# Flamingo block on one core: turned maxima ahead of the slot's extra products, values behind the first transposed scores, PSUM copies one slot later

## The chip, the cores and the metric

The kernel runs on one core of a Trainium2 chip. The metric is the device time of one execution in microseconds (us). The kernel before takes 424.69 us (median of 3 runs, 424.21 to 425.44).

## The reference

The input is `x` of 32 samples with 128 rows of 128 features, and for each sample a context of 77 rows. First a gated cross attention with 16 heads of 8 features, then a gated mixture of experts (one shared expert, and 3 of 15 routed ones for each row):

```python
query, key_, value = proj(layernorm(x), w_q), proj(ctx, w_k), proj(ctx, w_v)     # 16 heads of 8
attn = softmax(query @ key_.T / sqrt(8))
x = x + tanh(g_xattn) * ((attn @ value) merged @ w_o.T)
h = layernorm(x)
shared = gelu(h @ sW1 + sb1) @ sW2 + sb2
topv, topi = top_k(softmax(h @ gW + gb), 3)
routed = sum over the 3 chosen experts of topv * (gelu(h @ rW1[e] + rb1[e]) @ rW2[e] + rb2[e])
x = x + tanh(g_ffn) * (shared + routed + h)
```

## The kernel before

Each engine has an instruction stream written out by hand; semaphores tie them together. There is no scheduler: an engine does its instructions in the order of the code, and an instruction whose semaphore is not there yet holds up all behind it on that engine.

The first part is a loop over the 32 samples, one slot each: `for t in range(B)`, with `g, o = divmod(t, 4)`, so eight groups of four slots, o = 0 to 3. Each engine has its own copy of this loop. In slot t the core part of the attention is pipelined over several samples:

- TensorE (PE): `turn_max(t)` (L1315) transposes the row maxima of the scores of sample t into PSUM; `scores(t+1, 0..3)` (L1305) are the scores of the next sample, one product for each head group, in two PSUM banks used in turn; `turn_on` (L1358), `values(t-1)` (L1342), `scores_t(t, 0..3)` (L1325), the transposed scores of sample t with the maxima as further rows of one operand, also in two banks; `project(t-2)` (L1362), `turn_o(t-1)` (L1353).
- ScalarE (ACT): `max_rows(t)` (L695) copies the turned maxima out of PSUM into `q_stack`, where `scores_t(t, ..)` reads them; `exps(t, 0..3)` (L703); `onT_leaves`, `oT_leaves`.
- VectorE (DVE): `maxima(t+1, 0..3)` (L894) of the scores, on which `turn_max(t+1)` waits; `residual(t-2)` (L911), `invert`, `normalise`, `stats2_of`.

Beside this core each slot has extras, which differ with o. On PE: o = 0 `front_v(g+1)` (L1280) and `token_logits(g-2)` (L1381); o = 1 `front_x(g+2)` (L1263, in the middle of the slot) and `front_q(g+2)` (L1270); o = 2 `front_k(g+2)` (L1254) and `ranks(g-2)` (L1390 to L1394); o = 3 `turn_x2(g-1)` (L1373). Their results are copied out of PSUM by ACT (`lead_q` L668, `lead_k` L655, `x2T_leaves` L686) and DVE (`trail_q` L881, `trail_k` L877, `v_leaves` L887, `add_bias` L931, `place` L963). SyncE (SP) sends q and k to DRAM once they are complete (`send_q`, `send_k`) and loads them back in another layout for the group after next (`load_k`, `load_q` L381).

Two more chains pass through the loop. The second layer norm: `var2_of(g-1)` (L920, DVE), `pow2(g-1)` (L542 and L544, GpSimd (POOL), a power of -1/2) and `shift2_of(g-1)` (L927, DVE), the last two in slot o = 2; `shift2_of` stands ahead of `maxima(t+1, 2)` on DVE. The weights of the first expert layer: nine pieces, in each of them `lead_w1` (L720, ACT), then on POOL `trail_w1`: a subtraction (L557) and the load of the piece after next (L562). A piece comes every third slot, at t = 3, 6, ..., 27.

POOL also scatters normalised rows to the experts' areas in DRAM (L551), three in a slot from the last slot of group 2 on. POOL's loop is, in order:

```python
if o == 3 and g + 3 < NG: pow1(g + 3)
if o == 2 and g >= 1: pow2(g - 1)
if s >= 0:
    pool.wait_ge(exp_done, t * HG + 1);       scatter(s, m, m + 1)
    pool.wait_ge(exp_done, t * HG + 2)
    pool.wait_ge(max_done, (t + 1) * HG + 3); scatter(s, m + 1, m + 2)
    pool.wait_ge(exp_done, t * HG + 4);       scatter(s, m + 2, m + 3)
if t % 3 == 0 and 1 <= t // 3 <= PIECES: trail_w1(t // 3 - 1)
```

The second scatter of a slot thus waits for `maxima(t+1, 2)`, the third for `exps(t, 3)`.

After the loop come 76 blocks of routed expert work (L1434 to L1464), the shared expert, and gathers on POOL (L618) that bring the experts' rows back.

Of the kernel before, what the change touches and what calls it, by code (L numbers as in the profile page):

```python
# [17 lines left out]
def flamingo_kernel(nc, x, ctxT, g_xattn, g_ffn, wqT, wkT, wvT, woT, w1_chunks, b1_cols, sW2, w2_experts, b2, sb2,  # L18
                    gW, gb, ident, picks, consts, out):
    B, S, D = x.shape  # L20
# [10 lines left out]
    NG = B // GB  # L31
# [20 lines left out]
    ROUTE = 11  # L52
    PIECES = -(-NCH // 4)
    TABLE_AT = HALF * GB + 9

# [5 lines left out]
    with ExitStack() as ctx:  # L61
# [149 lines left out]
        zeroed = sem("zeroed")  # L211
# [309 lines left out]
        def _(pool):  # L521
# [59 lines left out]
            for t in range(B):  # L581
                g, o = divmod(t, GB)
# [8 lines left out]
                if s >= 0:  # L591
# [3 lines left out]
                    if t < B - 1:  # L595
# [4 lines left out]
                        scatter(s, m + 2, m + 3)  # L600
                if t % 3 == 0 and 1 <= t // 3 <= PIECES:
                    trail_w1(t // 3 - 1)

# [46 lines left out]
        def _(act):  # L650
# [94 lines left out]
            for t in range(B):  # L745
                g, o = divmod(t, GB)
                ahead = g + 2 < NG
                max_rows(t)
                if t >= 2:
                    onT_leaves(t - 2)  # L750
                if t >= 1:
                    oT_leaves(t - 1)
                exps(t, 0)
                exps(t, 1)
                if o == 1 and ahead:
                    xT_leaves(g + 2)
                if o == 0 and ahead:
                    apply1(g + 2, 0, 2)
                if o == 3 and 1 <= g < NG:
                    apply2(g - 1, 2, GB)  # L760
                if t == 0:
                    lead_q(1)
                exps(t, 2)
                exps(t, 3)
                if t == 0:
                    act.wait_ge(q_lo_ready, 2)
                    act.dma_start(qd[1], q_parts[:].bitcast(F32)).then_inc(q_sent, 16)
                if o == 0 and ahead:
                    apply1(g + 2, 2, GB)
                if o == 1 and ahead:  # L770
                    lead_q(g + 2)
                if o == 1 and g >= 2:
                    exp_logits(g - 2)
                if o == 2 and ahead:
                    lead_k(g + 2)
                if o == 2 and 1 <= g < NG:
                    apply2(g - 1, 0, 2)
                if o == 3 and g >= 1:
                    x2T_leaves(g - 1)
                if t % 3 == 0 and 1 <= t // 3 <= PIECES:  # L780
                    lead_w1(t // 3 - 1)

# [18 lines left out]
            def pad_rows(h, e):  # L801
                row = act.value_load(pad_row[0:1, h * E + e:h * E + e + 1], min_val=0, max_val=2 * HALF_ROWS - BLK)
                act.dma_start(xd[bass.ds(row, BLK), :].rearrange("(p c) d -> p (c d)", c=BC), zeros[:, 0:BC * D]).then_inc(pads_in[h], 16)

            lead_rows(0)
            lead_rows(1)
# [46 lines left out]
        def _(dve):  # L853
# [211 lines left out]
            for t in range(B):  # L1065
                g, o = divmod(t, GB)
                ahead = g + 2 < NG
                if t + 1 < B:
                    maxima(t + 1, 0)
                    maxima(t + 1, 1)  # L1070
                if o == 0 and ahead:
                    shift1_of(g + 2)
                if o == 1 and g >= 2:
                    choose(g - 2)
                if o == 2 and 1 <= g < NG:
                    var2_of(g - 1)
                if o == 2 and g >= 2:
# [5 lines left out]
                if t >= 2:  # L1083
                    residual(t - 2)
                if o == 2 and 1 <= g < NG:
                    shift2_of(g - 1)
# [3 lines left out]
                if t == 0:  # L1090
                    trail_q(1)
                    dve.wait_ge(tanh_done, 1)
                if 1 <= t <= B:
                    invert(t - 1)
                    normalise(t - 1)
                if o == 0 and g < NG - 1:
                    v_leaves(g + 1)
                if o == 1 and ahead:
                    trail_q(g + 2)
                if o == 2 and ahead:  # L1100
                    trail_k(g + 2)
                if t >= 2:
                    stats2_of(t - 2)
                if o == 3 and g >= 2:
                    weigh(g - 2)
                if o == 2 and g >= 2:
                    place(g - 2)
                if o == 2 and g + 3 < NG:
                    stats1_of(g + 3)
                    var1_of(g + 3)  # L1110
                if t >= B - NX + 1:
                    stage(t - (B - NX + 1))
                if o == 0 and g >= 2:
                    add_bias(g - 2)
                if t in (TABLE_AT, TABLE_AT + 1):
# [133 lines left out]
        def _(pe):  # L1249
# [206 lines left out]
            def layer2(u):  # L1456
# [9 lines left out]
                ins.then_inc(l2_done, 1)  # L1466

            for t in range(B):
                g, o = divmod(t, GB)
                ahead = g + 2 < NG  # L1470
                turn_max(t)
                if t + 1 < B:
# [4 lines left out]
                if t >= 2:  # L1477
                    turn_on(t - 2)
                if o == 1 and g >= 2:
                    pe.wait_ge(route_step, (g - 2) * ROUTE + 1)  # L1480
                if o == 3 and g >= 2:
                    pe.wait_ge(route_step, (g - 2) * ROUTE + 7)
                if t >= 1:
                    values(t - 1)
                scores_t(t, 0)
                scores_t(t, 1)
                if o == 1 and ahead:
# [12 lines left out]
                if t >= 1:  # L1500
                    turn_o(t - 1)
                if o == 0 and g < NG - 1:
                    front_v(g + 1)
# [7 lines left out]
                if o == 2 and g >= 2:  # L1511
                    if g == 2:
                        pe.wait_ge(zeroed, 2)
                    ranks(g - 2)
# [137 lines left out]
```

## Time and profile before

| | |
|---|---|
| runs | 424.69 us median (424.21 to 425.44) |
| profiled execution | 424.94 us, span 422.8 us |
| PE busy | 373.8 us, 88% |
| DVE, ACT, POOL busy | 295.8, 275.1, 267.2 us |
| the loop over samples, first `turn_max` to the last | 24.0 to 190.2 us of the span |

Busy times of one engine say how much of the span it worked; the rows of a timeline give the start and length of each instruction (those alike in a row are merged, xN), and in brackets how long the engine had sat idle before it and which instruction ended that. A matmul's row reaches to its modelled end, so that PE's pace is read from start to start.

### The profile page before, as it was taken

The numbers are of one execution on the slowest core, as the hardware profiler recorded it, in microseconds if no ns is written. First come the engines' busy times: TensorE is split into PE (matmuls) and PEld (weight loads), VectorE is DVE, ScalarE is ACT, GpSimd is POOL, SyncE is SP. The second block draws the span as 40 slices with busy tenths as digits, with TensorE's granted clock in tenths as the row PEclk, the third lists the DMA queues.
The fourth block names the chain that finished last, engine by engine and source line by source line (L and its number), as shares of the span: only waits on it lengthen the run. The fifth ranks groups of instructions, "written<-read, shape, count | busy, mean of one in ns | idle before, by whom it ended". The sixth has DMA issues, their size and how long they took to land.

```text
span 422.8 us, 12465 instructions
## 1 busy us (share of the span) xinstructions
PE 373.8 (88%) x3840; PEld 333.6 (79%) x3840; DVE 295.8 (70%) x968; ACT 275.1 (65%) x609; POOL 267.2 (63%) x263
## 2 busy tenths in 40 slices
PE   3379899989999989999899988899999999999940
PEld 1257778778787878877899987799999997999930
DVE  4546767687878768776668977678767762687862
ACT  4248799889889877977666654466666666354400
POOL 8920313357868767774987987406777776777771
PEclk9859999999999999999999999999999999999985
DMA  4457865638373637744345547656666652224232
GB/s 127 128 132 203 275 156 165 193 96 232 112 210 116 190 102 233 272 140 153 118 159 175 150 139 225 220 173 187 198 196 188 194 156 82 76 76 106 76 79 63
DMA packets 57463, 66.30 MB, mean 157 GB/s; under 512 B 9300, under 2 KB 48340, under 8 KB 57400
## 3 DMA queue, kind: packets, MB, share of 16 engines
q1 hardware_dynamic: 49224, 49.17, 39.3%
q0 software_dynamic: 6800, 14.46, 11.8%
q10 hardware_dynamic: 1376, 1.88, 1.4%
q8 instruction: 33, 0.54, 0.6%
q14 instruction: 30, 0.25, 0.2%
HBM read 35.63 MB, written 29.29 MB: 154 GB/s over the span
## 4 chain that ended last, share of the span: by engine, by line
PE 53%; POOL 16%; issue 7%; DMA 6%; DVE 5%; ACT 5%; SPq 3%; ACTq 2%; POOLq 0%; DVEq 0%
PE psum L1464 13%; POOL k_heads L618 8%; PE psum L1325 8%; PE psum L1342 6%; PE psum L1444 4%; PE psum L1445 3%; PE psum L1446 3%; PE psum L1305 3%; PE psum L1434 3%; POOL q_stack L618 2%; ACT probs L703 2%; DMA q_stack<-q_split 2%; DVE max_cols L894 2%; DMA w_raw<-rows_by_expert 2%; POOL rstd L544 2%
## 5 line engine op out<-in xcount | busy, mean ns | idle before, releaser
L551 POOL DMA_INDIRECT rows_by_expert<-xn_all,row_of x96 | 95.3, 993 | 35.7 <-issue 19.0
L798 ACT ACTIVATE probs<-psum,b1c 128x256 f32<-128x256 f32 x152 | 63.7, 470 | 26.3 <-PE psum L1446 25.4
L1464 PE MATMUL psum<-w_all,probs 128*128 x608 | 80.1, 275 | 0.0
L1464 PEld LDWEIGHTS psum<-w_all,probs 128*128 128x128 f32 x608 | 74.2, 191 | 0.2
L703 ACT ACTIVATE probs<-psum 77x512 f32<-77x512 f32 x128 | 68.8, 587 | 5.9 <-PE psum L1325 4.5
L618 POOL DMA_INDIRECT k_heads<-outs_by_block,back_row x60 | 58.3, 972 | 22.0 <-issue 16.2
L894 DVE TENSOR_REDUCE max_cols<-psum 128x4 fp32r<-128x312 f32 x128 | 55.2, 472 | 9.5 <-PE psum L1305 9.4
L1325 PE MATMUL psum<-q_stack,k_heads 128*77 128x128 f32 x512 | 55.1, 244 | 1.5 <-ACT q_stack L695 1.4
L1325 PEld LDWEIGHTS psum<-q_stack,k_heads 128*77 128x77 f32 x512 | 43.7, 150 | 14.5 <-issue 6.1
L1032 DVE CAST w_ring<-w 128x512 fp32r x76 | 34.7, 456 | 22.1 <-issue 20.6
L1444 PE MATMUL psum<-q_parts,w_ring 128*128 128x256 f32 x152 | 49.0, 323 | 1.1 <-DVE q_parts L1020 1.1
L787 ACT ACTIVATE q_parts<-psum 128x256 fp32r<-128x256 f32 x76 | 29.0, 384 | 27.2 <-PE psum L1434 26.7
L1305 PE MATMUL psum<-k_heads,q_stack 128*128 128x312 f32 x128 | 35.3, 357 | 9.8 <-DMA q_stack<-q_parts 6.7
L1445 PE MATMUL psum<-q_parts,w_ring 128*128 128x256 f32 x152 | 42.7, 281 | 0.0
L1446 PE MATMUL psum<-q_parts,w_ring 128*128 128x256 f32 x152 | 42.7, 281 | 0.0
L1020 DVE TENSOR_TENSOR q_parts<-psum,q_parts 128x256 fp32r<-128x256 f32 x76 | 31.8, 420 | 11.6 <-ACT q_parts L787 9.1
L618 POOL DMA_INDIRECT v_pad<-outs_by_block,back_row x24 | 23.5, 980 | 23.8 <-DMA outs_by_block<-probs 15.1
L1040 DVE TENSOR_TENSOR probs<-psum,probs 128x256 f32<-128x256 f32 x76 | 31.9, 420 | 7.3 <-PE psum L1464 3.1
L1342 PE MATMUL psum<-probs,v_pad 128*32 128x128 f32 x1024 | 34.6, 276 | 2.1 <-DVE placed L963 1.9
L1434 PE MATMUL psum<-ident_sb,w_raw 128*128 128x128 f32 x152 | 29.7, 278 | 5.7 <-DMA w_raw<-rows_by_expert 5.6
L1342 PEld LDWEIGHTS psum<-probs,v_pad 128*32 128x32 f32 x1024 | 26.0, 109 | 8.5 <-issue 4.5
L1580 PEld LDWEIGHTS psum<-w_shared,probs 128*128 128x128 f32 x256 | 29.7, 192 | 0.6
(151 smaller groups left out, 777.6 us busy)
## 6 DMA issues: line engine op xcount, KB each, us to landing
w_raw<-rows_by_expert SPq DMA_DIRECT2D x76, 128.0 KB
outs_by_block<-probs SPq DMA_DIRECT2D x76, 128.0 KB
q_stack<-q_split SPq DMA_DIRECT2D x21, 256.0 KB
k_heads<-k_split SPq DMA_DIRECT2D x90, 39.0 KB
rows_by_expert<-zeros SPq DMA_DIRECT2D x27, 128.0 KB, 3.8
q_split<-q_parts SPq DMA_DIRECT2D x6, 512.0 KB
k_split<-w_all SPq DMA_DIRECT2D x8, 312.0 KB, 2.4
x_all<-in_x SPq DMA_DIRECT2D x8, 256.0 KB, 4.6
```

The source lines that it names most:

```text
L551: nc.gpsimd.indirect_dma_start(xd[:, :], bass.IndirectOffsetOnAxis(ap=row_of[:, r, m:m + 1], axis=0), xn2_all[:, r * GB + m // K, :], None ...
L618: nc.gpsimd.indirect_dma_start(back[j][:, k * GB + b, :], None, yd[half][:, :], bass.IndirectOffsetOnAxis(ap=back_row[:, j, b * K + k:b * ...
L703: nc.scalar.activation(probs[0:KV, n % 2, hg * 512:(hg + 1) * 512], st_ps[hg % 2][0:KV, :], ACT.Exp, scale=SCALE).then_inc(exp_done, 1)
L798: nc.scalar.activation(hid[u % 2][:, c, :], psum[:, 2 + c, 0:BLK], ACT.Gelu, bias=b1c[:, bass.ds(e * CR + (CS + c), 1)]).then_inc(gelu_don ...
L894: nc.vector.tensor_reduce(max_cols[:, n % 2, hg * HQ:(hg + 1) * HQ], s_ps[hg % 2][:, 0:HQ * KP].rearrange("q (h k) -> q h k", h=HQ), AX.X, ...
L1305: nc.tensor.matmul(s_ps[hg % 2][:, 0:HQ * KP].rearrange("q (h k) -> q h k", h=HQ), q_stack[:, g % 2, hg, b * S:(b + 1) * S], k_heads[:, g ...
L1325: ins = nc.tensor.matmul(st_ps[hg % 2][0:KV, hh * S:(hh + 1) * S], k_heads[:, g % 2, hg, hh, b, 0:KV], q_stack[:, g % 2, hg, b * S:(b + 1) ...
L1342: ins = nc.tensor.matmul(a_ps[c * 32:(c + 1) * 32, half * S:(half + 1) * S], v_pad[:, g % 2, at:at + 32], probs[:, n % 2, h * S:(h + 1) * ...
L1444: nc.tensor.matmul(ps, w1_now[u % NX][:, 0, c, :], xs_hi[u % 2], start=True, stop=False)
L1445: nc.tensor.matmul(ps, w1_now[u % NX][:, 0, c, :], xs_lo[u % 2], start=False, stop=False)
L1446: nc.tensor.matmul(ps, w1_now[u % NX][:, 1, c, :], xs_hi[u % 2], start=False, stop=True).then_inc(l1_done, 1)
L1464: ins = nc.tensor.matmul(psum[:, 4 + u % 2 * 2, b * P:(b + 1) * P], hid[u % 2][:, c, b * P:(b + 1) * P], w2_all[:, bass.ds(expert_of[u] * ...
```

## The change

On PE `turn_max(t+1)` now stands at the end of slot t behind `turn_o(t-1)`, ahead of the extras, where it was at the start of slot t+1 behind them; the first two `scores_t` of a slot stand ahead of `values(t-1)`. On ACT `oT_leaves` follows the first two `exps`, and `lead_q`, `lead_k`, `exp_logits`, `x2T_leaves` move from the end of a slot to the next slot, behind `max_rows`. On DVE `v_leaves`, `trail_q`, `trail_k`, `place` and `add_bias` move into the next slot, around the first two `maxima`; `var2_of` moves from slot o = 2 to the end of slot o = 1. The nine pieces of the first expert layer's weights are put at the slots of a table `W1_AT`.

```diff
+    W1_AT = (3, 5, 9, 13, 17, 21, 25, 27, 28)
 # POOL
-                if t % 3 == 0 and 1 <= t // 3 <= PIECES:
-                    trail_w1(t // 3 - 1)
+                if t in W1_AT:
+                    trail_w1(W1_AT.index(t))
 # ACT
                 max_rows(t)
+                if o == 2 and ahead:
+                    lead_q(g + 2)
+                if o == 2 and g >= 2:
+                    exp_logits(g - 2)
+                if o == 3 and ahead:
+                    lead_k(g + 2)
+                if o == 0 and g >= 2:
+                    x2T_leaves(g - 2)
                 if t >= 2:
                     onT_leaves(t - 2)
+                exps(t, 0)
+                exps(t, 1)
                 if t >= 1:
                     oT_leaves(t - 1)
-                exps(t, 0)
-                exps(t, 1)
...
-                if o == 1 and ahead:
-                    lead_q(g + 2)
...
-                if o == 2 and ahead:
-                    lead_k(g + 2)
...
-                if t % 3 == 0 and 1 <= t // 3 <= PIECES:
-                    lead_w1(t // 3 - 1)
+                if t in W1_AT:
+                    lead_w1(W1_AT.index(t))
 # DVE
+                if o == 1 and g >= 2:
+                    add_bias(g - 2)
                 if t + 1 < B:
                     maxima(t + 1, 0)
                     maxima(t + 1, 1)
+                if o == 3 and g >= 2:
+                    place(g - 2)
+                if o == 1 and g < NG - 1:
+                    v_leaves(g + 1)
+                if o == 2 and ahead:
+                    trail_q(g + 2)
+                if o == 3 and ahead:
+                    trail_k(g + 2)
...
-                if o == 2 and 1 <= g < NG:
-                    var2_of(g - 1)
...
                 if t >= 2:
                     stats2_of(t - 2)
+                if o == 1 and g >= 1:
+                    var2_of(g - 1)
 # PE
+            turn_max(0)
             for t in range(B):
-                turn_max(t)
                 if t + 1 < B:
                     scores(t + 1, 0)
                     scores(t + 1, 1)
...
                 if t >= 2:
                     turn_on(t - 2)
+                scores_t(t, 0)
+                scores_t(t, 1)
...
                 if t >= 1:
                     values(t - 1)
-                scores_t(t, 0)
-                scores_t(t, 1)
...
                 if t >= 1:
                     turn_o(t - 1)
+                if t + 1 < B:
+                    turn_max(t + 1)
```

PE at the end of slot o = 2 and in slot o = 3 of group 3 (t = 14 and 15). `psum<-ident_r,max_cols` are the turned maxima, `psum<-w_all 128x312` is `front_k`, the three lines with `chosen` are `ranks`. Before:

```order
L1353 MATMUL psum<-ident_sb,oT 128x128 x2
L1254 MATMUL psum<-w_all 128x312
L1390 MATMUL psum<-chosen,after_r 128x64
L1391 MATMUL psum<-chosen,ones_r 128x64
L1394 MATMUL psum<-chosen,ones_r 128x48
L1394 MATMUL psum<-chosen,ones_r 128x32
L1394 MATMUL psum<-chosen,ones_r 128x16
L1315 MATMUL psum<-ident_r,max_cols 4x128 x4
L1305 MATMUL psum<-k_heads,q_stack 128x312 x2
L1358 MATMUL psum<-ident_sb,on 128x128
L1342 MATMUL psum<-probs,v_pad 32x128 x16
L1325 MATMUL psum<-q_stack,k_heads 77x128 x8
```

The same place now:

```order
L1355 MATMUL psum<-ident_sb,oT 128x128 x2
L1317 MATMUL psum<-ident_r,max_cols 4x128 x4
L1256 MATMUL psum<-w_all 128x312
L1392 MATMUL psum<-chosen,after_r 128x64
L1393 MATMUL psum<-chosen,ones_r 128x64
L1396 MATMUL psum<-chosen,ones_r 128x48
L1396 MATMUL psum<-chosen,ones_r 128x32
L1396 MATMUL psum<-chosen,ones_r 128x16
L1307 MATMUL psum<-k_heads,q_stack 128x312 x2
L1360 MATMUL psum<-ident_sb,on 128x128
L1327 MATMUL psum<-q_stack,k_heads 77x128 x8
L1344 MATMUL psum<-probs,v_pad 32x128 x16
```

The turned maxima have moved ahead of the extras, and the transposed scores ahead of the values.

POOL from the second scatter of slot t = 13 (o = 1, group 3) on. `rstd<-var` behind `var<-mv` with line L542/L544 is `pow2`, `w<-w_raw,w` and `w_raw<-in_w_chunks` are `trail_w1`. Before:

```order
L551 DMA rows_by_expert<-xn_all,row_of 131072x128 [waits max_done,exp_done]
L551 DMA rows_by_expert<-xn_all,row_of 131072x128 [waits exp_done]
L542 TENSOR_SCALAR var<-mv 128x4 [waits xn2_ready,ln2_step]
L544 TENSOR_TENSOR rstd<-var,half_pow 128x4 [waits var2_ready]
L551 DMA rows_by_expert<-xn_all,row_of 131072x128 [waits exp_done]
```

The same place now:

```order
L552 DMA rows_by_expert<-xn_all,row_of 131072x128 [waits max_done,exp_done]
L552 DMA rows_by_expert<-xn_all,row_of 131072x128 [waits exp_done]
L558 TENSOR_TENSOR w<-w_raw,w 128x512 [waits w1_lead]
L563 DMA w_raw<-in_w_chunks 128x512 [waits w1_ready]
L543 TENSOR_SCALAR var<-mv 128x4 [waits xn2_ready,ln2_step]
L545 TENSOR_TENSOR rstd<-var,half_pow 128x4 [waits var2_ready]
L552 DMA rows_by_expert<-xn_all,row_of 131072x128 [waits exp_done]
```

A piece of the weights now stands between the scatters of slot o = 1 and `pow2`; in the kernel before this was so at t = 9 and 21 alone, now it is so at t = 5, 9, 13, 17, 21 and 25.

DVE in slot t = 14 (o = 2). `shift<-mv,rstd` is `shift2_of`, which needs `pow2`. Before:

```order
L894 TENSOR_REDUCE max_cols<-psum 128x4 [waits s_done]
L920 BN_AGGR mv<-stats 128x2 [waits stats2_done]
L920 BN_AGGR mv<-stats 128x2 x3
L955 TENSOR_TENSOR picked<-con,top_at 128x180 [waits route_step]
L959 TENSOR_REDUCE chosen<-picked 128x4x15 [waits route_step]
L911 SCALAR_TENSOR_TENSOR x_all<-psum,tanh_g,x_all 128x128 [waits wo_done]
L927 SCALAR_TENSOR_TENSOR shift<-mv,rstd 128x4 [waits xn2_ready,ln2_rstd]
L894 TENSOR_REDUCE max_cols<-psum 128x4 [waits s_done] x2
```

The same place now:

```order
L896 TENSOR_REDUCE max_cols<-psum 128x4 [waits s_done]
L883 TENSOR_TENSOR q_parts<-psum,q_parts 128x512 [waits q_hi_ready]
L957 TENSOR_TENSOR picked<-con,top_at 128x180 [waits route_step]
L961 TENSOR_REDUCE chosen<-picked 128x4x15 [waits route_step]
L913 SCALAR_TENSOR_TENSOR x_all<-psum,tanh_g,x_all 128x128 [waits wo_done]
L929 SCALAR_TENSOR_TENSOR shift<-mv,rstd 128x4 [waits xn2_ready,ln2_rstd]
L896 TENSOR_REDUCE max_cols<-psum 128x4 [waits s_done] x2
```

The statistics (`mv`) have left this slot for the end of the one before, the copy of q has come in, and `shift2_of` still stands ahead of the last two maxima.

## Rows read from the trace of the kernel before

**Rows 1.** The page: span, and busy time of the engines.

```profile
span 422.8 us, 12465 instructions
PE 373.8 (88%) x3840; PEld 333.6 (79%) x3840; DVE 295.8 (70%) x968; ACT 275.1 (65%) x609; POOL 267.2 (63%) x263
```

**Rows 2.** Waits, whole span: us in total, times, longest us.

```profile
PEld psum L1325 <- issue: 6.1, 27, 0.6
PEld psum L1315 <- DVE max_cols L894: 4.6, 9, 1.0
```

**Rows 3.** Timeline of PE, slots t = 21 and 22: start us, length us, instruction, idle.

```profile
140.67 0.77 PE L1325 MATMUL psum<-q_stack,k_heads 128*77 128x128 f32 x8
141.28 0.62 PE L1263 MATMUL psum<-ident_sb,w_all 128*128 128x128 f32 x4
141.74 0.39 PE L1362 MATMUL psum<-w_oT,onT 128*128 128x128 f32 x2
141.88 0.54 PE L1305 MATMUL psum<-k_heads,q_stack 128*128 128x312 f32 x2
142.26 0.71 PE L1325 MATMUL psum<-q_stack,k_heads 128*77 128x128 f32 x8
142.80 0.40 PE L1353 MATMUL psum<-ident_sb,oT 128*128 128x128 f32 x2
143.04 1.02 PE L1270 MATMUL psum<-w_all 128*128 128x512 f32 x2
143.50 0.80 PE L1315 MATMUL psum<-ident_r,max_cols 128*4 128x128 f32 x4
144.14 0.51 PE L1305 MATMUL psum<-k_heads,q_stack 128*128 128x312 f32 x2
...
144.69 1.08 PE L1342 MATMUL psum<-probs,v_pad 128*32 128x128 f32 x32
146.03 0.77 PE L1325 MATMUL psum<-q_stack,k_heads 128*77 128x128 f32 x8 [0.26 <-ACT q_stack L695]
...
148.49 0.69 PE L1254 MATMUL psum<-w_all 128*128 128x312 f32 x2
...
150.56 0.40 PE L1315 MATMUL psum<-ident_r,max_cols 128*4 128x128 f32 x4 [0.92 <-DVE max_cols L894]
...
151.88 1.08 PE L1342 MATMUL psum<-probs,v_pad 128*32 128x128 f32 x32 [0.46 <-DVE placed L963]
```

**Rows 4.** Timeline of DVE, slots t = 21 and 22.

```profile
142.43 0.86 DVE L894 TENSOR_REDUCE max_cols<-psum 128x4 fp32r<-128x312 f32 x2
...
146.60 0.83 DVE L955 TENSOR_TENSOR picked<-con,top_at 128x180 f32<-128x180 f32 x1
...
149.56 0.16 DVE L927 SCALAR_TENSOR_TENSOR shift<-mv,rstd 128x4 f32<-128x4 f32 x1 [1.46 <-POOL rstd L544]
149.64 0.87 DVE L894 TENSOR_REDUCE max_cols<-psum 128x4 fp32r<-128x312 f32 x2
```

**Rows 5.** Timeline of POOL, slots t = 21 and 22.

```profile
143.68 0.96 POOL L551 DMA_INDIRECT rows_by_expert<-xn_all,row_of  x1 [0.45 <-ACT probs L703]
144.94 0.96 POOL L551 DMA_INDIRECT rows_by_expert<-xn_all,row_of  x1 [0.30 <-issue]
145.92 1.29 POOL L557 TENSOR_TENSOR w<-w_raw,w 128x512 fp32r<-128x512 f32 x1
...
148.49 1.04 POOL L544 TENSOR_TENSOR rstd<-var,half_pow 128x4 f32<-128x4 f32 x1
```

**Rows 6.** Timeline of SP in group 1: the sending of k, the last loads of q.

```profile
64.07 0.33 SPq L340 DMA_DIRECT2D k_split<-w_all  x1
...
73.04 2.29 SPq L381 DMA_DIRECT2D q_stack<-q_split  x3
```

**Rows 7.** Timeline of PE, the turned maxima of t = 11.

```profile
85.14 0.40 PE L1315 MATMUL psum<-ident_r,max_cols 128*4 128x128 f32 x4 [0.67 <-DVE max_cols L894]
```

**Rows 8.** Timeline of DVE, the same line as in rows 4 in slot t = 14.

```profile
103.82 0.31 DVE L955 TENSOR_TENSOR picked<-con,top_at 128x180 f32<-128x180 f32 x1
```

More of the change, by code:

```diff
@@ L758, in _ @@
                     apply1(g + 2, 0, 2)
-                if o == 3 and 1 <= g < NG:
+                if o == 3 and g >= 1:
                     apply2(g - 1, 2, GB)
@@ L769, in _ @@
                     apply1(g + 2, 2, GB)
-                if o == 1 and ahead:
-                    lead_q(g + 2)
-                if o == 1 and g >= 2:
-                    exp_logits(g - 2)
-                if o == 2 and ahead:
-                    lead_k(g + 2)
-                if o == 2 and 1 <= g < NG:
+                if o == 2 and g >= 1:
                     apply2(g - 1, 0, 2)
-                if o == 3 and g >= 1:
-                    x2T_leaves(g - 1)
-                if t % 3 == 0 and 1 <= t // 3 <= PIECES:
-                    lead_w1(t // 3 - 1)
+                if t in W1_AT:
+                    lead_w1(W1_AT.index(t))
             def lead_rows(u):
@@ L803, in pad_rows @@
                 act.dma_start(xd[bass.ds(row, BLK), :].rearrange("(p c) d -> p (c d)", c=BC), zeros[:, 0:BC * D]).then_inc(pads_in[h], 16)
+            x2T_leaves(NG - 2)
             lead_rows(0)
@@ L1074, in _ @@
                     choose(g - 2)
-                if o == 2 and 1 <= g < NG:
-                    var2_of(g - 1)
                 if o == 2 and g >= 2:
@@ L1084, in _ @@
                     residual(t - 2)
-                if o == 2 and 1 <= g < NG:
+                if o == 2 and g >= 1:
                     shift2_of(g - 1)
@@ L1092, in _ @@
                     dve.wait_ge(tanh_done, 1)
-                if 1 <= t <= B:
+                if t >= 1:
                     invert(t - 1)
                     normalise(t - 1)
[L1096 to L1101, printed above, removed]
                 if t >= 2:
                     stats2_of(t - 2)
+                if o == 1 and g >= 1:
+                    var2_of(g - 1)
                 if o == 3 and g >= 2:
                     weigh(g - 2)
-                if o == 2 and g >= 2:
-                    place(g - 2)
                 if o == 2 and g + 3 < NG:
@@ L1112, in _ @@
                     stage(t - (B - NX + 1))
-                if o == 0 and g >= 2:
-                    add_bias(g - 2)
                 if t in (TABLE_AT, TABLE_AT + 1):
@@ L1511, in _ @@
                 if o == 2 and g >= 2:
-                    if g == 2:
-                        pe.wait_ge(zeroed, 2)
                     ranks(g - 2)
```

## The prediction

> **What bounds the kernel now.** I read the page first: PE is busy 88% of 422.8 us, no other engine over 70% [rows 1]. That says only that the order of PE's work matters. The change is confined to the loop over samples, so I went to PE's timeline there and took its pace from start to start. One slot (t = 21, o = 1) shows the parts [rows 3]: two `scores_t` 0.61 (140.67 to 141.28), `front_x` 0.46, `project` 0.14, two `scores` 0.38, two more `scores_t` 0.54, `turn_o` 0.24, `front_q` 0.46, `turn_max` behind it 0.64 (drain of the long product included), two `scores` and `turn_on` 0.55, `values` 1.08. PE runs nearly without a gap; what it loses it loses in short waits. The waits view gives those that the change aims at [rows 2]: 27 stalls of 0.23 before `scores_t` (6.1 in all; the second pair stands too close behind the first, whose bank is not yet read by `exps`), and 4.6 us before `turn_max` on the maxima. Single ones in the timeline: 0.26 on the copy of the maxima, 0.92 on the maxima, 0.46 on `place` [rows 3], 0.67 on the maxima at t = 11 [rows 7].
>
> The 0.92 is the row to read. It names DVE, but DVE had itself idled 1.46 us before `shift2_of`, waiting for POOL [rows 4], and POOL had worked through, back to back, the second scatter at 143.68, the third, the weights' piece (L557), its load, and only then `pow2`, which ends at 148.49 + 1.04 = 149.53 [rows 5]. So in this slot the loop is bound by a POOL queue: 5.85 us from the second scatter to the end of `pow2`, then 1.03 more until the turned maxima start at 150.56. This happens with a piece in slot o = 1. Before, that is t = 9 and t = 21.
>
> **The change, part by part.** The profiled execution takes 424.94 us, 2.1 more than its span, and 0.25 more than the median of the runs; the sum is made against 424.94.
>
> *Order on PE.* With `values` between the first transposed scores and the second, `exps` gets 1.08 us more than now: the 0.23 stalls go, three in a group (the slot with `front_x` has none), -0.7 a group. `turn_max(t+1)` loses its cover. Counted from the start of `project`, it is next in line after 0.14 + 0.38 + 0.54 + 0.24 = 1.30. The maxima it needs end at 142.43 + 0.86 = 143.29, that is 1.55 after `project` at 141.74 [rows 3, 4], and start it 0.05 later. New wait: 0.3 in every slot, where today the extras (0.46 to 1.7 us) hide it; three slots of a group +0.9, the fourth (o = 2) comes below. In return `max_rows` gets the extras as cover, and the 0.26 waits go, one each in groups 2, 4 and 5: -0.2 each. `place` moves behind the first two maxima of the slot; PE waits for it ahead of `values`, now later in the slot. I leave its 0.46 almost as it is (0.40): the maxima it stands behind can't start before PE's own `scores`. Bounds: none, or 0.9 if it comes behind a late DVE.
>
> *Pieces.* The table puts six of nine pieces at o = 1, on POOL right ahead of the next slot's `pow2`; DVE's `shift2_of` stands ahead of the last two maxima of slot o = 2, and PE's `turn_max` behind these now has no extras ahead of it. Walk for groups 3 to 5, which have three scatters in a slot, from the start of the first `scores_t` in slot o = 1. `project` starts at 0.61 + 1.08 + 0.46 = 2.15. The second scatter waits for the third quarter of the maxima, which starts 0.69 behind `project` and ends some 0.45 later (a little over half of the pair's 0.86), so it starts at 3.34. `pow2` ends 5.85 later, at 9.19. The slot itself lasts 0.61 + 1.08 + 0.46 + 0.14 + 0.38 + 0.54 + 0.24 + (0.46 + 0.64) + 0.55 = 5.10, and 0.30 of wait: 5.40. So `pow2` ends 3.79 into slot o = 2 and `turn_max` starts 1.03 later, at 4.82. PE is there at 0.61 + 1.08 + 0.14 + 0.38 + 0.54 + 0.24 = 2.99. Wait: 1.8 us. Bounds: 0.3 (if `pow2` were early, as in any slot) and 0.92 + 1.15 = 2.07, today's wait at t = 22 and the `front_k` and `ranks` ahead of it (148.49 to 149.64, where the idle begins) that are then no cover. I take 1.8, the walked value. That `var2_of` goes a slot earlier doesn't help: `pow2` waits for its place in POOL's queue, not for the statistics. What queues behind: DVE's last maxima, `invert`, `normalise`; ACT's `apply2`; PE entirely.
>
> Groups then change by: group 3, +1.8 + 0.9 - 0.7 = +2.0; group 4, the same less a 0.2 wait on `max_rows`, +1.8; group 5 loses also today's 0.92, +0.9. Groups 1 and 2 have a piece at o = 1 without scatters before it, so the chain is shorter; group 2 pays 0.67 for it today [rows 7], with the extras as cover. I put +0.4 on each (from -0.5, all waits gone, to +1.2, when the 1.15 of products no longer covers). In group 6 there are no q and k extras, so slot o = 1 is shorter by some 1.3 us and `pow2` reaches further into the next: by the same walk 2.7, less some 0.5 for the expert-table steps that lengthen these slots: 2.2; `place` behind the late DVE +0.5; the pieces at t = 27 and 28, one right after the other on ACT and POOL, +0.4: +3.1 (1.5 to 4). Groups 0 and 7: +0.2, the first bound by loads.
>
> *Copies later.* `lead_q`, `lead_k` and their trailing parts go to the next slot, so `send_q` and `send_k` leave SP up to half a slot (2.5 us) later, and all loads queued behind on SP with them. In group 1 k is sent at 64.07 and the last load of q is issued by 73.04 + 2.29 = 75.33 [rows 6]; it is needed at the first scores of group 3, behind the turned maxima at 85.14 [rows 7]: 9.8 us of cover, of which 2.5 go. Cost 0; if it did not cover, up to 2.5 a group. ACT's and DVE's instructions are the same in number and length; ahead of `exps` they fall beside PE's products.
>
> One rule on contention: the match that marks the chosen experts took 0.83 us at 146.60 while POOL's subtraction ran (145.92 to 147.21), and 0.31 at 103.82 without [rows 4, 5, 8]. The Trainium skill (SBUF — State Buffer, section "SBUF: two separate sides") says that VectorE and GpSimd share one pair of ports as an exclusive lock, and that a VectorE instruction with two SBUF inputs is fully blocked until the other ends; the trace agrees, 0.5 us. By that rule the change puts the subtraction of four more groups beside this match and would add up to 2 us. By the rows it ends before DVE's wait for `pow2` and adds nothing.
>
> Sum: 0.4 + 0.4 + 2.0 + 1.8 + 0.9 + 3.1 + 0.2 = +8.8, 433.7 for the profiled execution, less 0.25: **433.5 us**. What follows the loop (expert blocks on PE, then gathers) starts as much later and isn't changed.
>
> **Rivals.**
> 1. *The reorder wins.* The waits of rows 2 go (-6.1 - 4.6), the new one of 0.3 stands in some 24 slots (+7.2), and `pow2` is not late: 424.7 - 3.5 = 421.2. It wants POOL to reach `pow2` a full 1.8 us earlier. For: PE has the highest busy share and POOL 63%. Against: rows 5, POOL without a gap in just this slot. The Trainium skill (Perfetto Trace Analysis, "Identifying the Most-Contended Engine") says to close the gaps of the engine with the highest occupancy; by that rule PE's waits are worth their whole sum; the trace shows them set elsewhere.
> 2. *A wash.* As forecast, but the chain ends 1.1 us earlier in the five slots o = 2 of groups 2 to 6 (the second scatter not held by the maxima), and groups 1 and 2 come out even, and group 6 pays 1: 433.5 - 5.5 - 0.8 - 2.1 = 425.
> 3. *More than that.* The loads of q and k are late too, 1 us in each of groups 3 to 6: 437.5. Against: 7.3 us of cover left.
>
> **How the numbers follow.** Forecast 0.80, rival 1 0.08, rival 2 0.07, rival 3 0.05. The forecast's own range goes from 429.3 (wait of 1.2, group 6 at 1.5, groups 1 and 2 at 0) to 436.8 (wait of 2.07, group 6 at 4, groups 1 and 2 at 1.2). The range that holds 8 in 10: 427.5 to 437. A measurement tells about 0.3% (1.3 us) from no change: faster 0.07, same 0.05, slower 0.88.
>
> **What would show it.** Right: PE idle of 1.5 to 2 us before the turned maxima at the end of slots t = 14, 18, 22, 26, named as DVE's maxima, DVE idle before `shift2_of` put down to POOL, and there scatter, scatter, subtraction, load, power without a gap; 0.2 to 0.3 before the turned maxima elsewhere; no more stalls of `scores_t` on `exps`. Wrong: `shift2_of` without idle, or turned maxima that start on time; then rival 1 or 2. Idle before scores put down to a DMA speaks for rival 3.

## The result, and the profile after

The changed kernel takes 439.82 us (median of 4, 439.06 to 440.23) against 424.68 us on the same chip (424.21 to 425.44): a ratio of 1.035, interval 1.0331 to 1.0369. It is slower, as forecast, and by 6.3 us more than the 433.5 forecast: 2.8 us above the top of the range. The profiled execution is the fastest of the four, and the mean granted clock of the other three is lower (0.945 to 0.948 against 0.955), so what the profile shows of the clock is the least of it. Its page (439.06 us), with the clock line of the 40 slices:

```profile
span 437.1 us, 12464 instructions
PE 377.0 (86%) x3840; PEld 338.2 (77%) x3840; DVE 299.9 (69%) x968; ACT 274.8 (63%) x609; POOL 266.4 (61%) x263
PEclk9769999999999969889999999999999999999995
```

The span grew by 14.3 us [rows 1] and PE's busy time by 3.2. In slice 15 and in slices 17 and 18 (10.9 us each), all inside the loop, the granted clock isn't full.

The waits view (PEld is TensorE's loading of weights, which overlaps its products; line numbers are one or two higher than before, so that L1325 is now L1327 and L1315 is L1317):

```profile
PEld psum L1327 <- issue: 1.1, 2, 0.6
PEld psum L1317 <- DVE max_cols L896: 19.4, 29, 2.1
PEld psum L1327 <- ACT q_stack L696: 7.9, 17, 2.3
```

Against [rows 2]: the stalls of `scores_t` on "issue" are down from 27 to 2, and the turned maxima wait 29 times where they waited 9 times. The same slots t = 21 and 22 as in [rows 3], on PE:

```profile
144.89 0.79 PE L1327 MATMUL psum<-q_stack,k_heads 128*77 128x128 f32 x8
...
148.18 0.41 PE L1355 MATMUL psum<-ident_sb,oT 128*128 128x128 f32 x2
148.72 0.40 PE L1317 MATMUL psum<-ident_r,max_cols 128*4 128x128 f32 x4
...
150.35 0.77 PE L1327 MATMUL psum<-q_stack,k_heads 128*77 128x128 f32 x8
151.05 1.08 PE L1344 MATMUL psum<-probs,v_pad 128*32 128x128 f32 x32
...
153.61 0.41 PE L1355 MATMUL psum<-ident_sb,oT 128*128 128x128 f32 x2 [0.23 <-DVE x_all L913]
155.93 0.59 PE L1317 MATMUL psum<-ident_r,max_cols 128*4 128x128 f32 x4 [1.90 <-DVE max_cols L896]
156.31 1.35 PE L1256 MATMUL psum<-w_all 128*128 128x312 f32 x2
```

DVE and POOL there, beside [rows 4, 5]:

```profile
151.68 1.12 DVE L957 TENSOR_TENSOR picked<-con,top_at 128x180 f32<-128x180 f32 x1
...
154.93 0.16 DVE L929 SCALAR_TENSOR_TENSOR shift<-mv,rstd 128x4 f32<-128x4 f32 x1 [1.46 <-POOL rstd L545]
155.01 0.86 DVE L896 TENSOR_REDUCE max_cols<-psum 128x4 fp32r<-128x312 f32 x2
```

```profile
150.31 0.95 POOL L552 DMA_INDIRECT rows_by_expert<-xn_all,row_of  x1 [0.30 <-issue]
151.28 1.29 POOL L558 TENSOR_TENSOR w<-w_raw,w 128x512 fp32r<-128x512 f32 x1
...
153.85 1.04 POOL L545 TENSOR_TENSOR rstd<-var,half_pow 128x4 f32<-128x4 f32 x1
```

The chain is the forecast one: POOL works through scatter, piece, load and `pow2`, DVE waits 1.46 us, PE 1.90. Slot 14 has the same: 1.91 us before its turned maxima at 108.55. Look at the last PE row above: `front_k` lasts 1.35 us, where one such product pair took 0.69 before [rows 3]. That is the clock. The windows view of after, by slots (busy time of each engine, then the granted clock, DMA share, GB/s): slot 14, slot 18, slots 22 and 23, slots 26 and 27.

```profile
102.96:110.25 7.29, 5.14 (x69) 4.37 (x69) 5.72 (x20) 5.19 (x12) 6.17 (x7) 1.00 0.40 138
126.66:133.93 7.27, 5.14 (x69) 4.37 (x69) 5.71 (x20) 5.19 (x12) 6.18 (x7) 1.00 0.38 135
150.35:159.11 8.76, 6.63 (x70) 5.61 (x69) 4.70 (x13) 5.20 (x12) 7.14 (x8) 0.79 0.35 123
159.11:165.17 6.06, 5.92 (x67) 4.86 (x66) 4.07 (x15) 4.11 (x10) 1.84 (x2) 0.75 0.25 87
...
176.04:184.63 8.59, 6.21 (x76) 5.40 (x75) 5.97 (x17) 4.45 (x10) 7.04 (x9) 0.88 0.81 295
184.63:191.91 7.28, 6.60 (x67) 5.68 (x65) 4.36 (x18) 4.74 (x11) 2.65 (x4) 0.67 0.14 46
```

Where the mean is between 0.5 and 1 the clock stood at 1.2 GHz for a part of the slot and at 2.4 for the rest; the rows of PE show the first. In slot 27 `values` takes 1.94 us, one slot earlier 1.08:

```profile
176.74 1.08 PE L1344 MATMUL psum<-probs,v_pad 128*32 128x128 f32 x32
...
185.95 1.94 PE L1344 MATMUL psum<-probs,v_pad 128*32 128x128 f32 x32
```

Before, the clock is 1.00 in the slots 22, 23, 26 and 27:

```profile
146.03:152.89 6.86, 5.41 (x68) 4.40 (x69) 5.29 (x19) 4.84 (x11) 5.64 (x7) 1.00 0.42 149
152.89:157.61 4.72, 4.69 (x70) 3.79 (x66) 3.31 (x13) 4.53 (x10) 3.17 (x4) 1.00 0.35 109
167.75:172.81 5.06, 5.06 (x79) 4.56 (x75) 4.45 (x21) 4.16 (x9) 4.13 (x6) 1.00 1.02 397
172.81:177.59 4.78, 4.75 (x69) 3.79 (x66) 3.80 (x14) 4.59 (x11) 3.43 (x4) 1.00 0.66 225
```

So two things were open: what the waits would have cost with the clock up, and how the loss divides between the pieces and the order of the queues.

### The profile page after: what moved, and what is told of

Same layout as the page of the kernel before. It is cut to its first block, busy times and chain, and to the rows that moved or that the text cites. A ratio compares the mean times of both kernels' runs of the same rounds, so it can differ in the third digit from the quotient of the medians.

```text
span 437.1 us, 12464 instructions
## 1 busy us (share of the span) xinstructions
PE 377.0 (86%) x3840; PEld 338.2 (77%) x3840; DVE 299.9 (69%) x968; ACT 274.8 (63%) x609; POOL 266.4 (61%) x263
## 4 chain that ended last, share of the span: by engine, by line
PE 47%; POOL 19%; issue 8%; DVE 8%; ACT 6%; DMA 5%; SPq 4%; ACTq 2%; POOLq 0%; DVEq 0%
PE psum L1466 12%; POOL k_heads L619 8%; PE psum L1344 6%; PE psum L1327 4%; DVE max_cols L896 4%; PE psum L1446 3%; PE psum L1447 3%; PE psum L1448 3%; PE psum L1436 3%; ACT probs L704 3%; PE psum L1307 2%; POOL rows_by_expert L552 2%; POOL q_stack L619 2%; PE psum L1364 2%; POOL w L558 2%
## 5 line engine op out<-in xcount | busy, mean ns | idle before, releaser
L704 ACT ACTIVATE probs<-psum 77x512 f32<-77x512 f32 x128 | 68.7, 587 | 15.1 <-PE psum L1327 14.8
L1327 PE MATMUL psum<-q_stack,k_heads 128*77 128x128 f32 x512 | 50.2, 242 | 4.2 <-ACT q_stack L696 4.2
L1327 PEld LDWEIGHTS psum<-q_stack,k_heads 128*77 128x77 f32 x512 | 45.2, 154 | 9.7 <-ACT q_stack L696 7.9
L1307 PE MATMUL psum<-k_heads,q_stack 128*128 128x312 f32 x128 | 39.0, 386 | 9.0 <-DMA q_stack<-q_parts 7.6
L1344 PE MATMUL psum<-probs,v_pad 128*32 128x128 f32 x1024 | 36.3, 285 | 1.4 <-DVE placed L965 1.4
L1307 PEld LDWEIGHTS psum<-k_heads,q_stack 128*128 128x128 f32 x128 | 21.5, 204 | 13.0 <-issue 10.2
L1344 PEld LDWEIGHTS psum<-probs,v_pad 128*32 128x32 f32 x1024 | 27.2, 113 | 4.3 <-DVE placed L965 1.9
```

What stands on the lines that cost most here:

```text
L704: nc.scalar.activation(probs[0:KV, n % 2, hg * 512:(hg + 1) * 512], st_ps[hg % 2][0:KV, :], ACT.Exp, scale=SCALE).then_inc(exp_done, 1)
L1307: nc.tensor.matmul(s_ps[hg % 2][:, 0:HQ * KP].rearrange("q (h k) -> q h k", h=HQ), q_stack[:, g % 2, hg, b * S:(b + 1) * S], k_heads[:, g ...
L1327: ins = nc.tensor.matmul(st_ps[hg % 2][0:KV, hh * S:(hh + 1) * S], k_heads[:, g % 2, hg, hh, b, 0:KV], q_stack[:, g % 2, hg, b * S:(b + 1) ...
L1344: ins = nc.tensor.matmul(a_ps[c * 32:(c + 1) * 32, half * S:(half + 1) * S], v_pad[:, g % 2, at:at + 32], probs[:, n % 2, h * S:(h + 1) * ...
```

## The experiments

Each time stands beside runs of the kernel before on the same chip: 424.73 us for e1 to e4, 424.2 for e5 to e8, 424.12 for e9 and e10. "Slot 14" is the time from the first `scores_t` of t = 14 to that of t = 15.

**e1: the pieces back at their old places, all else as changed.**

```diff
-    W1_AT = (3, 5, 9, 13, 17, 21, 25, 27, 28)
+    W1_AT = (3, 6, 9, 12, 15, 18, 21, 24, 27)
```

> The changed kernel with the pieces of the weights back at every third slot (t = 3, 6, ..., 27), all else as changed. Theory (the pieces ahead of the power on POOL hold the loop, and the long idle that follows lets the clock fall): a piece at o = 1 is left at t = 9 and 21 alone, so the waits of 1.9 us before the turned maxima go at t = 14 and 18 and stay at t = 10 and 22; at t = 26 the wait falls below 1 us. One stretch at the lower clock at most, after t = 22. Time 428 to 432 us. Rival (the order on PE, with the turned maxima ahead of the extras, is what costs): no change from 439.8, within 2 us.

430.15 us (428.16 to 431.59), ratio 1.0124, 1.0068 to 1.018. Slots 14, 18 and 26 are 5.32, 5.84 and 5.65 us instead of 7.29, 7.28 and 8.59. The one slot o=2 that still follows a piece at o=1 (t=21) is slot 22, with 7.29 us and the old wait:

```profile
152.94 0.40 PE L1317 MATMUL psum<-ident_r,max_cols 128*4 128x128 f32 x4 [1.91 <-DVE max_cols L896]
```

In the profiled execution the clock doesn't fall after it, nor anywhere else in the loop. At t = 10, where the old wait was expected as well, it is 0.79. So 9.7 of the 15.1 us lost go with the new places of the pieces, a part of the change that its title doesn't name.

**e2: the kernel before with the new table alone.** Its only edit is `W1_AT` of the changed kernel.

> The kernel before with only the table of pieces put in (t = 3, 5, 9, 13, 17, 21, 25, 27, 28). Theory: POOL reaches the power late in slots t = 14, 18, 22 and 26; the extras ahead of the turned maxima cover 1.2 us of it, so the idle there is 0.7 to 0.9 us as it is at t = 22 today, and some 1.7 at t = 26 where the q and k products are missing; no stretch at the lower clock beyond those of before. Time 427 to 430 us. Rival (order on PE): 424.7, within 1 us. If the table were the whole loss whatever the order, 437 or more.

431.52 us (429.96 to 434.05), ratio 1.0167, 1.0108 to 1.0226: 1.5 us above the range. Slots 14, 18, 22 and 26 are 6.88, 7.30, 7.14 and 7.09. PE's wait before the turned maxima is 0.93 us in the first three, as expected and half of the 1.90 in the changed kernel, so the extras ahead of them do cover about 1 us:

```profile
107.51 0.40 PE L1316 MATMUL psum<-ident_r,max_cols 128*4 128x128 f32 x4 [0.93 <-DVE max_cols L895]
```

In slot 26 PE waits 1.07 us ahead of `turn_o` and 0.50 ahead of the turned maxima. The table alone costs 6.8 us, the other moves without it 5.4 (e1), both together 15.1: some 3 us more than the two apart. The expectation had the clock stay up; it fell twice in the loop, in slots 18 and 19 and in 22 and 23:

```profile
125.63:132.94 7.31, 5.85 (x69) 4.65 (x69) 5.74 (x26) 4.86 (x11) 6.09 (x7) 0.93 0.50 173
132.94:138.25 5.31, 5.31 (x69) 4.88 (x65) 3.75 (x15) 4.69 (x10) 4.07 (x6) 0.77 0.24 72
149.32:156.46 7.14, 5.67 (x68) 4.47 (x68) 5.32 (x19) 4.86 (x11) 5.92 (x7) 0.96 0.49 173
156.46:161.95 5.49, 5.49 (x69) 5.06 (x65) 3.05 (x13) 4.74 (x10) 2.97 (x4) 0.74 0.24 76
```

**e3: `pow2` on POOL ahead of the piece.**

```diff
-                if o == 2 and g >= 1:
-                    pow2(g - 1)
...
+                if o == 1 and g >= 1:
+                    pow2(g - 1)
                 if t in W1_AT:
```

> The changed kernel with the power on POOL moved from the head of slot o = 2 to slot o = 1, behind the three scatters and ahead of the piece (subtraction and load, 2.2 us). Theory: the power ends 2.2 us earlier, the idle before the turned maxima of t = 14, 18, 22, 26 falls from 1.9 to about 0.3, no stretch at the lower clock in the loop after 42 us; 5 slots gain 1.5 us and the two low stretches give back some 5: 425 to 429 us. If only the clock mattered and not the queue, the idle stays; if the order on PE costs, 437 or more.

431.38 us (430.73 to 432.35), ratio 1.0144, 1.0103 to 1.0185. That is 8.4 us less than the changed kernel, but 2.4 above the range. PE's wait before the turned maxima is 1.17 us in slots 14, 18 and 22 and 1.40 in slot 26, not 0.3; slots 14, 18 and 22 are 6.14. The clock was expected to stay up, and fell once in the loop, behind the wait of slot 26. DVE and POOL in slot 14 show why the wait is still there:

```profile
105.16 1.11 DVE L929 SCALAR_TENSOR_TENSOR shift<-mv,rstd 128x4 f32<-128x4 f32 x1
106.19 0.86 DVE L896 TENSOR_REDUCE max_cols<-psum 128x4 fp32r<-128x312 f32 x2
```

```profile
103.94 1.05 POOL L545 TENSOR_TENSOR rstd<-var,half_pow 128x4 f32<-128x4 f32 x1
104.98 1.26 POOL L558 TENSOR_TENSOR w<-w_raw,w 128x512 fp32r<-128x512 f32 x1
```

`shift2_of` no longer waits for POOL, but it now runs beside the piece and takes 1.11 us in place of 0.16. It ends within 0.03 us of the piece. The wait became a collision.

**e4: PE kept busy in the wait.** In slots o=2 of groups 3 to 6, behind `turn_o`, eight products that nothing uses:

```diff
+                if o == 2 and 3 <= g < NG - 1:
+                    pe.wait_ge(m_ready, t + 1)
+                    for _ in range(8):
+                        nc.tensor.matmul(psum[:, 4, 0:P], w_oT[:], ident_sb[:], start=True, stop=True)
                 if t + 1 < B:
                     turn_max(t + 1)
```

> The changed kernel with eight more products of 128 x 128 (some 1.5 us of PE) ahead of the turned maxima in slots o = 2 of groups 3 to 6; their result isn't used, and they fill the idle time without ending it. The theory that the long idle brings the clock down, and that this costs about 5 us beside the waits: the granted clock stays at its upper level after 42 us, slots t = 22, 23, 26 and 27 fall by about 1 us each or more, 434 to 437 us though PE does more work. If the clock follows something else (the whole chip, the time): both low stretches stay, 439.8 or a little more.

435.49 us (435.23 to 437.42), ratio 1.0259, 1.0211 to 1.0307: 4.3 us faster than the changed kernel for more work. The waits themselves are still paid: slots 14 and 18 are 7.29 each. The clock isn't lost:

```profile
150.41:157.71 7.30, 6.93 (x86) 6.20 (x85) 4.70 (x12) 5.21 (x12) 6.19 (x7) 1.00 0.39 138
157.71:162.90 5.19, 4.58 (x68) 3.77 (x66) 4.08 (x15) 4.07 (x10) 2.79 (x3) 1.00 0.31 109
173.77:181.64 7.87, 7.01 (x93) 6.51 (x91) 5.69 (x14) 4.46 (x10) 6.34 (x8) 1.00 0.89 335
181.64:187.75 6.11, 4.61 (x67) 3.76 (x65) 4.72 (x19) 4.58 (x11) 2.99 (x4) 1.00 0.17 58
```

Slots 22, 23, 26 and 27 are 1.46, 0.87, 0.72 and 1.17 us shorter (8.76, 6.06, 8.59, 7.28 against 7.30, 5.19, 7.87, 6.11): together 4.2, about the difference of the medians (the spans of the two profiled executions differ by 3.4, since what follows the loop took 0.8 longer here). Over all runs the mean clock is 0.962 to 0.969 here and 0.945 to 0.955 in the changed kernel.

**e5: DVE's maxima ahead of `shift2_of`** in slots o=2, the pieces left at o=1.

```diff
-                if o == 2 and g >= 1:
-                    shift2_of(g - 1)
                 if t + 1 < B:
                     maxima(t + 1, 2)
                     maxima(t + 1, 3)
+                if o == 2 and g >= 1:
+                    shift2_of(g - 1)
```

> The changed kernel with one step of DVE moved: in slots o=2 `shift2_of` stands behind `maxima` of heads 2 and 3 and no longer ahead of them. The pieces stay at o=1. Theory: the long slots o=2 come from one chain alone, piece and scatters on POOL, then `pow2`, then DVE's `shift2_of`, behind which the maxima stand in DVE's queue; so with the maxima ahead of it the waits of 1.9 us before the turned maxima fall to some 0.3, the slots 14 to 15, 18 to 19 and 22 to 23 go from 7.29, 7.28 and 8.75 to 5.3 to 6.2, the clock stays at 1.00 in the loop, and the time comes to 428.5 to 432 us, as with the pieces at their old places (430.15). Rival: `shift2_of` only hands the lateness on, to `normalise` behind it on DVE and to `apply2` on ACT, and so to the turned rows on PE: 434 to 438. Second rival: the fall of the clock has nothing to do with these waits and comes all the same: above 433 with two stretches at half clock in the loop.

430.14 us (429.78 to 430.71), ratio 1.0142, 1.0105 to 1.0178: as expected. PE's wait before the turned maxima is 0.28 us in slot 14 and in slot 26. Slots 14, 18 and 22 are 6.35, 6.32 and 6.33, a little over the expected 6.2. So the chain to PE runs through `shift2_of`. A part of the lateness is handed on, as the rival had it: in slot 14 ACT idles 0.93 us for `shift2_of`, and PE 0.44 for the copied maxima behind that; with 0.25 before `turn_o` this is most of the 1.03 us by which the slot is longer than in e1. In slot 26 PE waited 0.87 us for `residual` ahead of `turn_o`, behind a match of 2.12 us on DVE. The clock fell once in the loop, in slots 26 and 27, which was not expected, with no wait recorded in slot 26 that is longer than this:

```profile
169.68:176.46 6.78, 5.63 (x76) 4.70 (x75) 5.91 (x16) 4.46 (x10) 5.54 (x8) 0.97 0.96 367
176.46:183.05 6.59, 5.89 (x67) 4.80 (x66) 4.48 (x18) 4.64 (x11) 3.81 (x5) 0.77 0.25 86
```

**e6: the pieces in slots o=0** from group 3 on: `W1_AT = (3, 6, 8, 10, 12, 16, 20, 24, 28)`.

> The changed kernel with the pieces at t = 3, 6, 8, 10, 12, 16, 20, 24, 28, so from group 3 on in slots o=0, where no second power follows on POOL. Theory: a piece is dear only in a slot o=1. With the pieces at their old places one of them (t=21) was still there, and the slot behind it was 7.29 us beside 5.3 to 5.8 in the other groups; without it that slot goes to 5.3 to 5.8 too: 1.7 us less than the 430.15 of that run, 426.5 to 430 us, clock 1.00 in the loop. Rival: a piece costs its POOL time wherever it stands, since the scatters behind it come later and the marks and gathers with them: 430 to 433. What is left above 424.7 is the price of the new order of the queues alone.

426.4 us (425.49 to 429.46), ratio 1.0056, 1.003 to 1.0082: just under the range. Slot 22 is 5.31. The pieces' places, with the clock that went with them, are the 13.4 us between this and the changed kernel. The 2.2 us left above the kernel before aren't the price of the order alone, since the kernel before still has a piece at t = 21: with its table the order costs 5.4 (e1).

**e7: e1 with the turned maxima back at the head of the slot**, as in the kernel before.

> The changed kernel with the pieces at their old places (t = 3, 6, ... 27) and, beside that, the turned maxima back at the head of the slot; all other moves of the queues stay. Theory: the move of the turned maxima is about a wash, since the stalls of 0.23 us that it takes from the transposed scores stand against a new wait of some 0.3 us on DVE's maxima: 429 to 432 us against 430.15 with the move. Rival: the move is what the new order costs, and without it the time is back at that of the kernel before, 424 to 426 us. Third: the move is a gain that the other moves eat, and without it the time is 433 to 436 us.

428.12 us (427.71 to 429.75), ratio 1.0104, 1.0066 to 1.0143: 2.0 less than e1, 0.9 below the "wash". The turned maxima seem better off behind the extras, but the intervals of e1 and e7 overlap, so the gain isn't shown. What is shown is the price of the other moves: 3.9 us above the kernel before, with the same table and the turned maxima in the same place.

**e9: both together,** the pieces of e6 and the turned maxima at the head.

> The changed kernel with both undone: the pieces at t = 3, 6, 8, 10, 12, 16, 20, 24, 28 and the turned maxima at the head of the slot. What is left of the change are the other moves: values behind the first transposed scores, the copies of the extra products a slot later. Theory: they cost nothing, since they have 9.8 us of cover; the pieces' places and the place of the turned maxima are the whole change. From 426.4 (pieces at o=0) less the 2.0 that the head was worth with the old pieces (430.15 to 428.12): 424.4, so 423.4 to 425.4 us. Rival: the 2.0 was the scatter between runs or hung on the piece at t=21, and the time stays at 426 to 427. Second rival: the other moves are a gain, and the time is under 423.

425.3 us (423.21 to 426.46), ratio 1.0014, 0.9988 to 1.0041: no difference from the kernel before, and in the expected range. But this doesn't show that the moves left in it cost nothing, since e9 has no piece at t = 21: slot 22 is 5.30 us here, 6.66 in e7 and 6.86 in the kernel before. With this table the total is even; with the old one (e7) the same moves cost 3.9 us. PE's waits show where, e9 first, then the kernel before:

```profile
PE psum L1327 <- ACT q_stack L696: 12.0, 31, 2.0
```

```profile
PE psum L1325 <- ACT q_stack L695: 1.4, 4, 0.7
```

With `values` behind the first `scores_t`, nothing stands between the turned maxima and the products that need their copy, and PE waits for it in 31 slots (12.4 us in e7). The copies a slot later weren't tried by themselves. Against e6 the head gains 1.1 us, less than the expected 2.0, and the two kernels' times overlap.

**e8: another version.** The kernel before with no piece at o=1 from group 2 on, `place` on DVE sooner, and `turn_o` on PE between the last two transposed scores.

```diff
+    W1_AT = (3, 6, 8, 10, 12, 14, 18, 22, 26)
...
                     normalise(t - 1)
+                if o == 2 and g >= 2:
+                    place(g - 2)
...
-                scores_t(t, 3)
                 if t >= 1:
                     turn_o(t - 1)
+                scores_t(t, 3)
```

> The kernel before with three other moves: pieces at t = 3, 6, 8, 10, 12, 14, 18, 22, 26, so never in a slot o=1 from group 2 on; `place` on DVE right behind `normalise` in slots o=2, ahead of `trail_k` and `stats2_of`; and `turn_o` on PE between the transposed scores of heads 2 and 3. Theory: the slot 22 to 23 of before (6.86 us beside 5.80 in the groups ahead of it, with its piece at t=21) goes to 5.8, which gives 1.1 us; `placed` comes some 0.4 us sooner, which the values of six slots o=3 wait for, up to 2.0 us; the transposed out-projection between the scores covers part of the stalls on `exps`, up to 1 us: 420.5 to 422.5 us. Rival: the waits only change places (DVE's statistics late, ACT's copies late), and the time is 424 to 426 us. Second rival: a piece at o=2 sits ahead of scatters that feed the gathers, 426 to 429 us.

420.62 us (418.51 to 423.69), ratio 0.9916, 0.9886 to 0.9946: within the range, and 0.8% faster than the kernel before.

**e10: e8 with `turn_o` back in its place.**

> The faster other version (420.62) with `turn_o` on PE back behind the transposed scores of all four heads: the kernel before with the pieces out of the slots o=1 and `place` ahead of `trail_k`, both on other engines than PE. Theory: the piece at t=21 was worth 1.1 us and the earlier `placed` up to 2.0, `turn_o` between the scores up to 1: 421 to 423 us. Rival: `turn_o` between the scores gave it all, since it stands in all 31 slots, and the time is 424 to 425.

419.72 us (419.0 to 422.08), ratio 0.9922, 0.9894 to 0.9951, 1.3 us below the range, so `turn_o` gave nothing that can be measured and its share in the estimate for e8 was wrong. Slot 22 is 5.39 us instead of 6.86. That is the gain of both moves: the waits of 0.92 on the maxima and of 0.46 on `place` [rows 3] are gone, and PE waits hardly at all:

```profile
142.74:148.13 5.39, 5.29 (x72) 4.40 (x69) 4.74 (x19) 4.90 (x12) 3.95 (x6) 1.00 0.34 128
```

## Why the prediction was right in kind and too low

By groups, from the start of `scores_t` at their first slots, in us (the first row counts from the span's start to group 3, and the forecast for groups 0 and 7 is put in the last):

| | forecast | changed kernel | e4, clock kept |
|---|---|---|---|
| groups 0 to 2 | +0.8 | -0.5 | -0.4 |
| group 3 | +2.0 | +2.2 | +2.2 |
| group 4 | +1.8 | +2.4 | +2.5 |
| group 5 | +0.9 | +3.4 | +1.1 |
| group 6 | +3.1 | +6.8 | +4.9 |
| group 7 | +0.2 | +0.3 | +0.3 |
| sum | +8.8 | +14.6 | +10.5 |

**Right: the chain and its price.** The wait was put at 1.8 us and is 1.90 and 1.91. Both its ends came later than walked: `pow2` ended 10.00 us after the start of slot 21 (154.89 less 144.89), not 9.19; PE was ready 3.68 into slot 22, not 2.99. The errors cancel: that the wait came out within 0.1 us is luck. The first lies in the start of the second scatter: the walk has it 0.05 us behind the third quarter of the maxima, it is 0.78 in the changed kernel, and [rows 4, 5] show as much (maxima from 142.43, scatter at 143.68); the 5.85 us from there are right. The second is in part a wait of 0.23 before `turn_o` that the walk doesn't have. e1, e5 and e6 show the links: no piece at o=1, or no `shift2_of` ahead of the maxima, and the wait of 1.9 us is gone. Groups 3 and 4 are short by 0.2 and 0.6.

**Half right: the order on PE and the copies.** The stalls on "issue" went, and the new regular wait is there: in slot 21 the turned maxima start 0.54 us behind `turn_o` (148.18 to 148.72), where the next product started 0.24 behind it before [rows 3]. But the sum had the order at a net +0.2 a group and the copies at nothing. With the old table all these moves cost 5.4 us (e1), and 3.9 without the move of the turned maxima (e7). The sum has `values` between the transposed scores as a gain alone; that they were the cover for the copy of the maxima, 31 waits in e7 and e9, isn't in it. In the changed kernel the turned maxima come sooner and 6 such waits are left (4.2 us).

**Failed: "groups then change by".** The sum took each wait at its own length and every other row at its old duration, so it had no term for the clock. In the changed kernel the clock fell to 1.2 GHz at the waits of slots 22 and 26, and the products that follow took nearly twice as long. e4 measures this at 4.3 us, two thirds of the 6.3 missed. With the clock kept, the kernel takes 435.5, inside the range. The Trainium skill (TensorE: Matmul & The Clock Gate, section "HAM oscillation — how this bites in real kernels") describes a kernel in which TensorE stops for a DMA in every pass and starts the next piece of work with its clock down. The waits here are shorter than the 3 to 5 us of that kernel; the trace agrees all the same in slots 22 and 26, and doesn't in slots 14 and 18, where a wait of the same length left the clock at 1.00.

**Failed in size: group 6, +3.1.** With the clock kept it is +4.9. Slot 26 was put at +2.2 and is 2.8 longer (7.87 in e4 against 5.06), slot 27 at +0.9 and is 1.3 longer (6.11 against 4.78), with waits of 0.89 on `placed` and 0.47 on the copied maxima. Slot 25 was put at nothing and costs 0.7 (5.12 against 4.43), with new waits of 0.16 before `turn_o` and 0.28 before the turned maxima.

**Right here: contention "adds nothing".** The match that marks the chosen experts ran beside the piece in four slots. It took 1.12 to 1.13 us in three of them and 2.12 in slot 26, instead of 0.31 [rows 8]. DVE and POOL in slot 26:

```profile
176.82 2.12 DVE L957 TENSOR_TENSOR picked<-con,top_at 128x180 f32<-128x180 f32 x1
...
181.08 0.16 DVE L929 SCALAR_TENSOR_TENSOR shift<-mv,rstd 128x4 f32<-128x4 f32 x1 [1.06 <-POOL rstd L545]
```

```profile
177.45 1.28 POOL L558 TENSOR_TENSOR w<-w_raw,w 128x512 fp32r<-128x512 f32 x1
```

Even after 2.12 us DVE idles 1.06 for POOL, so the turned maxima would not have started sooner; part of their wait only moves ahead of `turn_o`:

```profile
180.17 0.41 PE L1355 MATMUL psum<-ident_sb,oT 128*128 128x128 f32 x2 [0.88 <-DVE x_all L913]
182.08 0.41 PE L1317 MATMUL psum<-ident_r,max_cols 128*4 128x128 f32 x4 [1.50 <-DVE max_cols L896]
```

Where the chain through POOL is taken away, the collision shows: 0.87 us in slot 26 of e5, and e3's `shift2_of`. The Trainium skill's rule (SBUF — State Buffer, "SBUF: two separate sides"), that the later of the two instructions waits for the whole of the earlier, agrees with the trace in e3. In slot 26 the match is recorded 0.63 us ahead of the piece and still ends 0.21 behind it, which that rule alone doesn't explain. It began while a scatter was running on POOL (176.46 to 177.42); so it did in e2, e4 and e5 (2.02 to 2.12 us), while beside a scatter without a piece behind it the match takes 0.31 to 0.40 (the kernel before, e1, e3, e6).

**Open.** Why the clock falls at some of these waits and not at others of equal length (slots 14 and 18 of the changed kernel, slot 22 of e1), and in slots 26 and 27 of e3 and e5 after shorter ones. That PE's idle time brings it down in slots 22 and 26 is shown by e4, where the waits stay as long as they were and only the idle time in them is filled; one of e4's four runs (437.42 us, mean clock 0.962) may still have had a fall. Which of the other moves costs the 3.9 us of e7 wasn't separated.

## What to carry to other kernels

Price a slow step by where it stands in its engine's queue: here a 1.3 us subtraction on an engine with 61% busy time cost the most, because `pow2` stood behind it and a chain over two more engines behind that. A wait on TensorE can cost more than its length, so give a forecast of several new waits of about 2 us a second term, for products at the lower clock behind them. A product that is moved may have been the cover for something else: ask what ran behind it. And when a wait is moved away, look at what now runs side by side: in e3 the wait for GpSimd came back as a VectorE instruction that GpSimd held up.

## What the runs showed of the hardware

- The granted clock fell in the middle of a loop at two of four waits of about 2 us, and `values` went from 1.08 to 1.94 us. Eight unused products in each of the four waits bought back 4.3 us.
- A VectorE instruction of 0.31 us took up to 2.12 us beside GpSimd's subtraction, and one of 0.16 us took 1.11.
